# The edge matrix of a graph network, built in 56 groups of 14 packets of edges in place of 98 groups of 8

## What is computed

```python
edge_index = jnp.stack([src, dst])
h = relu(layernorm(x)); x = x + L0(h, edge_index, ...)      # two attention (GAT) layers, 4 heads
h = relu(layernorm(x)); x = x + L1(h, edge_weight, ...)     # 3 Lanczos steps: w = segment_sum(edge_weight * v[src], dst)
h = relu(layernorm(x)); x = x + L2(h, src, dst, ...)        # 3 SAGE layers: mean of h[src] over dst
h = relu(layernorm(x)); x = x + L3(h, edge_index, edge_type_16, ...)   # message passing with types
```

## Time and profile before

| | |
|---|---|
| median of 3 runs | 6159.81 us (6158.36 to 6174.29) |
| the profiled execution, its own time | 6145.26 us |
| its span, first to last instruction | 6143.5 us |
| mean granted TensorE clock | 0.691 |
| busy share of the span: PE, DVE, ACT, POOL | 50%, 51%, 29%, 62% |
| scatter of the matrix: first and last start | 234.3 and 1932.5 us |
| masks of the first attention layer | 1936 to about 2298 us |

### The profile page before, as it was taken

How to read it: one execution, slowest core, us unless ns; L and a number is a source line. 1 busy time by engine, 2 the same in 40 slices (tenths; PEclk the granted TensorE clock), 3 DMA queues, 4 the chain that set the end, 5 groups by cost and what they waited for, 6 DMA issues and landing times.

```text
span 6143.5 us, 54878 instructions
## 1 busy us (share of the span) xinstructions
PE 3078.6 (50%) x14893; PEld 1695.4 (28%) x14894; DVE 3122.8 (51%) x4163; ACT 1760.1 (29%) x2530; POOL 3806.0 (62%) x2603
## 2 busy tenths in 40 slices
PE   1311111111112556776434777699999934444444
PEld 0211111111111222221333222244445413333333
DVE  5455555444444998998798999611210051111111
ACT  0000000000001447998443999600111150000001
POOL 0377777777777888888787999810000007777774
PEclk6555555555555778999655999899999965555555
DMA  9422112222224974433897333487567642222222
GB/s 410 136 1 1 0 0 1 1 1 1 1 1 139 353 278 114 107 99 77 275 312 235 101 104 89 120 279 276 203 229 256 230 171 52 52 52 52 52 52 40
DMA packets 445350, 760.69 MB, mean 124 GB/s; under 512 B 273431, under 2 KB 351449, under 8 KB 405461
## 3 DMA queue, kind: packets, MB, share of 16 engines
q1 hardware_dynamic: 275280, 702.23, 33.7%
q0 software_dynamic: 163840, 54.71, 9.6%
q10 hardware_dynamic: 6146, 2.68, 0.2%
HBM read 552.67 MB, written 187.47 MB: 120 GB/s over the span
## 4 chain that ended last, share of the span: by engine, by line
issue 22%; PE 20%; POOL 18%; DVE 16%; DMA 15%; ACT 3%; POOLq 1%; SPq 1%; DVEq 0%; ACTq 0%
PE PS L636 17%; POOL edge_weight_and_count L579 12%; DVE tiles L1494 6%; POOL tiles L610 6%; DMA edge_weight_and_count<-weight_and_count,target 5%; DVE feature_major L1440 4%; DMA tiles<-edge_weight_and_count 4%; DVE tiles L1487 3%; DMA copies_then_records<-edge_count 3%; DMA tiles<-message_table,gather_index 2%; PE PS L756 1%; PE PS L945 1%; DMA message_table<-tiles 1%; ACT copies_then_records L1070 1%; DVE smax L1449 0%
## 5 line engine op out<-in xcount | busy, mean ns | idle before, releaser
L599 POOL DMA_INDIRECT sorted_edges<-record_slot,place_slot x784 | 1557.4, 1987 | 294.2 <-issue 212.1
L579 POOL DMA_INDIRECT edge_weight_and_count<-weight_and_count,target x784 | 1240.8, 1583 | 682.0 <-issue 251.0
L610 POOL DMA_INDIRECT tiles<-message_table,gather_index x808 | 774.9, 959 | 1274.4 <-DMA message_table<-tiles 1028.4
L636 PE MATMUL PS<-tiles,node_major 128*128 128x448 f32 (+1 forms) x2100 | 810.5, 546 | 10.7 <-ACT node_major L1001 10.7
L945 PE MATMUL PS<-tiles 128*128 128x128 f32 x1616 | 492.0, 460 | 614.1 <-DMA tiles<-message_table,gather_index 614.0
L636 PE MATMUL PS<-tiles 128*64 128x392 f32 (+1 forms) x3200 | 649.5, 528 | 292.9 <-DVE tiles L1494 290.8
L1494 DVE SCALAR_TENSOR_TENSOR tiles<-tiles,copies_then_records 128x1568 f32<-128x1568 f32 (+1 forms) x400 | 698.6, 1780 | 34.8 <-ACT tiles L1104 22.0
L1440 DVE SCALAR_TENSOR_TENSOR feature_major<-tiles,s,feature_major 128x1600 f32<-128x1600 f32 (+3 forms) x384 | 679.3, 1839 | 40.1 <-ACT tiles L1057 40.1
L945 PEld LDWEIGHTS PS<-tiles 128*128 128x128 f32 x1616 | 374.9, 322 | 731.7 <-issue 731.7
L1641 DVE TENSOR_TENSOR tiles<-lane_row,edges 128x1024 f32<-128x1024 f32 x101 | 123.5, 1225 | 881.4 <-PE PS L945 871.5
L636 PEld LDWEIGHTS PS<-tiles,node_major 128*128 128x128 f32 (+1 forms) x2100 | 400.5, 193 | 398.2 <-issue 383.2
(11 more groups left out here) (246 smaller groups left out, 3640.1 us busy)
## 6 DMA issues: line engine op xcount, KB each, us to landing
tiles<-edge_weight_turned SPq DMA_DIRECT2D x72, 1568.0 KB, 7.5
tiles<-edge_count SPq DMA_DIRECT2D x72, 1568.0 KB, 7.0
tiles<-edge_weight_and_count SPq DMA_DIRECT2D x48, 1600.0 KB
edge_weight_and_count<-tiles SPq DMA_DIRECT2D x48, 1568.0 KB, 39.3
copies_then_records<-edge_count SPq DMA_DIRECT2D x192, 392.0 KB
tiles<-edge_weight_and_count SPq DMA_DIRECT2D x48, 1536.0 KB, 8.7
edge_weight_turned<-copies_then_records SPq DMA_DIRECT2D x48, 768.0 KB, 4.8
edge_count<-copies_then_records SPq DMA_DIRECT2D x24, 800.0 KB, 4.1
```

Of the source, the lines that this page charges most:

```text
L579: nc.gpsimd.indirect_dma_start(out=edge_d, out_offset=bass.IndirectOffsetOnAxis(ap=idx[:, s, a:a + 1], axis=0), in_=pay[:, s, a, :], in_of ...
L599: nc.gpsimd.indirect_dma_start(out=rec_d, out_offset=bass.IndirectOffsetOnAxis(ap=place_slot[:, s, a:a + 1], axis=0), in_=rec_slot[:, s, a ...
L610: nc.gpsimd.indirect_dma_start(out=msg[:, s, a, :], out_offset=None, in_=table_d, in_offset=bass.IndirectOffsetOnAxis(ap=gs[:, s, a:a + 1] ...
L636: return nc.tensor.matmul(out_ap, lhsT, rhs, start=start, stop=stop)
```

## The change

The group size GB becomes 14 in all these places: 56 groups of 14 packets in place of 98 of 8. EC is still 784, so the 784 indirect DMAs of the matrix and the 784 of the sort stay. In a group the blocks are 14 * 15 / 2 = 105 in place of 36.

To fit two slots into the arrays, the blocks are stored as a folded triangle: row b (14 - b blocks) and row 13 - b (b + 1 blocks) share one strip of 15 blocks. The diagonal blocks then lie in two regular patterns, so the mask multiply becomes two instructions of 7 blocks each (`e.per = g + 2` signals a group in place of g + 1). One slot takes all of what was spare in `feature_major` from column 3 * 3136, the other starts at the front of `tiles`; so the zero tile, which SP reads while the first groups are made, moves to the array `Dinv`.

In PSUM a slot has four banks (1792 columns of keys, then `counted` and `summed` in the last 256 columns of its fourth bank). Packets 12 and 13 of a group's keys share that bank with the results of the group that used the slot before. So `key_rows` waits ahead of packet 12 for `edge_targets` of that group, and the tail waits for ScalarE's copy (`e.copied`) ahead of its first instruction in place of its third.

```diff
-GB, GM, GS = 8, 2, 8
+GB, GM, GS = 14, 2, 8
...
+        half, row, d = g // 2, (g + 1) * TP, g * TP
+        n = half * row
+        self.per = g + 2
+        self.words = (n + 2 * d) // 2
+        self.start = [b * row if b < half else (g - 1 - b) * row + (b + 1) * TP for b in range(g)]
+        self.diagonal_slot = [b if b < half else half + g - 1 - b for b in range(g)]
...
+        e0 = 8 * NP - 3 * ecp - 3 * ecp // 2
...
-        build_s = EdgeSteps(GB, [fm[0:TP, e1 + 3 * ecp // 2:8 * NP], tiles[0:TP, NP:3 * NP]], BF16, upto_b,
+        build_s = EdgeSteps(GB, [fm[0:TP, 3 * NP:e0], tiles[0:TP, :]], BF16, upto_b,
...
-        turned_keys = [bigT[0:TP, 8 * s:8 * s + 8, 0:TP] for s in range(2)]
-        counted = [BIG[0:TP, 6, 0:GB], SM[0:TP, 0:GB]]
+        turned_keys = [PS[0:TP, 4 * s:4 * s + 4, :].rearrange("p b (q n) -> p (b q) n", n=TP)[:, 0:GB, :] for s in range(2)]
+        counted = [PS[0:TP, 4 * s + 3, 256:256 + GB] for s in range(2)]
+        summed = [PS[0:TP, 4 * s + 3, 320:320 + 4 * GB] for s in range(2)]
...
-                    sp.dma_start(edge_m[t * TP:t * TP + n, k * NP:(k + 1) * NP], A[0][0:n, :]).then_inc(S("edges_cleared"), 16)
+                    sp.dma_start(edge_m[t * TP:t * TP + n, k * NP:(k + 1) * NP], Dinv[0:n, :]).then_inc(S("edges_cleared"), 16)
...
                 for a in range(e.g):
+                    if a == 12 and not (isinstance(i, int) and i < 2):
+                        pe.wait_ge(S(e.targets), i - 1 if isinstance(i, int) else before * 1)
                     last = nc.tensor.transpose(turned_keys[s][:, a, :],
...
-                    v.tensor_tensor(e.eqd[s], e.diagonal[s], e.upto[:, :].unsqueeze(1).to_broadcast([TP, e.g, TP]),
-                                    ALU.mult).then_inc(S(e.eq_done), 1)
+                    half = e.g // 2
+                    for k in range(2):
+                        v.tensor_tensor(e.eqd[s][:, k * half:(k + 1) * half, :], e.diagonal[s][k],
+                                        e.upto[:, :].unsqueeze(1).to_broadcast([TP, half, TP]), ALU.mult).then_inc(S(e.eq_done), 1)
...
+                    dve.wait_ge(S(e.copied), i + 1)
                     o(v.tensor_tensor(jk[:, s, 0:e.g], same[:, s, 0:e.g], counted[s][:, 0:e.g], ALU.subtract))
                     o(v.scalar_tensor_tensor(jk[:, s, 0:e.g], jk[:, s, 0:e.g], 1.0, junkD[:, at], ALU.min, ALU.mult))
-                    dve.wait_ge(S(e.copied), i + 1)
```

More of the change, by code:

```diff
@@ L158, in __init__, with columns @@
         self.targets, self.copied, self.added = targets, copied, added
[L159 to L162, removed]
+        half, row, d = g // 2, (g + 1) * TP, g * TP
[4 more added lines that the diff above has]
+        self.diagonal_slot = [b if b < half else half + g - 1 - b for b in range(g)]
+        self.flat, self.diagonal, self.eqd = [], [], []
         for a in areas:
-            a = a[:, 0:self.words] if dt == F32 else a[:, 0:self.words].bitcast(dt)
-            self.eq.append(a[:, 0:n].rearrange("p (b n) -> p b n", b=g))
-            self.diagonal.append(a[:, 0:n + d].rearrange("p (b n) -> p b n", b=g)[:, :, 0:TP])
+            a = a[:, 0:self.words].bitcast(dt)
+            self.flat.append(a[:, 0:n])
+            self.diagonal.append([a[:, 0:n].rearrange("p (i n) -> p i n", n=row)[:, :, 0:TP],
+                                  a[:, d:d + half * d].rearrange("p (i n) -> p i n", n=d)[:, :, 0:TP]])
             self.eqd.append(a[:, n + d:n + 2 * d].rearrange("p (b n) -> p b n", b=g))
+    def columns(self, s, b, first, last):
+        return self.flat[s][:, self.start[b] + (first - b) * TP:self.start[b] + (last - b) * TP]
 def graph_layers(nc, x, src, dst, etype, eweight, W1, as1, ad1, b1, W2, as2, ad2, b2, LW,
@@ L672, in to_feature_major, with key_rows @@
                 last.then_inc(S("fm_turned"), 1)
-            def key_rows(i, s, e):
+            def key_rows(i, s, e, before=None):
                 pe.wait_ge(S(e.loaded), i + 1)
                 for a in range(e.g):
+                    if a == 12 and not (isinstance(i, int) and i < 2):
+                        pe.wait_ge(S(e.targets), i - 1 if isinstance(i, int) else before * 1)
                     last = nc.tensor.transpose(turned_keys[s][:, a, :],
@@ L694, in sum_values @@
                     for b in range(a + 1):
-                        last = mm(BIG[0:TP, 4 + s, a * width:(a + 1) * width], e.eq[s][:, b, a * TP:(a + 1) * TP],
+                        last = mm(summed[s][:, a * width:(a + 1) * width], e.columns(s, b, a, a + 1),
                                   value(b), b == 0, b == a)
@@ L1304, in equal @@
                     for b in range(e.g):
[L1305 removed]
+                        v.tensor_scalar(e.columns(s, b, b, e.g).rearrange("p (a n) -> p a n", n=TP),
                                         turned_keys[s][:, b:e.g, :], ks[:, s, b:b + 1], None,
                                         ALU.is_equal, ALU.add, accum_out=same[:, s, b:b + 1]).then_inc(S(e.eq_done), 1)
[L1308 to L1310 removed]
+                    dve.wait_ge(S(e.eq_done), i * e.per + e.g)
+                    half = e.g // 2
+                    for k in range(2):
+                        v.tensor_tensor(e.eqd[s][:, k * half:(k + 1) * half, :], e.diagonal[s][k],
+                                        e.upto[:, :].unsqueeze(1).to_broadcast([TP, half, TP]), ALU.mult).then_inc(S(e.eq_done), 1)
                 def body(i, s, first):
```

21 lines of the change are left out of this document (11 added, 10 removed).

## The result

The changed kernel takes 6136.2 us (median of 20 runs, 6097 to 6171) where the kernel before takes 6190.0 (20 runs, 6150 to 6229, these beside it). The ratio is 0.9919, 95% interval 0.9900 to 0.9937: by the ratio 50 us, or 0.8%, faster, and 54 between the medians. Forecast was 42.

A forecast was written before the change was run, and what follows sets the result against it. GpSimd's scatter packets and the landing waits between groups were taken as the bound. Fewer group changes -86.5, later first group +22.5 and collisions +22 gave -42 us: 6118 us on the 6159.8 median, range 6086 to 6152.

The forecast's parts named there:

- What bounds the stage: Matrix scatter, 234 to 1933 us: GpSimd's packets and landing waits set the time; other engines cost nothing unless they delay GpSimd.
- the 40 us that the sum for the stage before left over: Scatter before: time beyond packets and group changes, put down to long gaps (21 us) and bucket work (15 us).
- Changes of group: GpSimd's scatter: 42 fewer group changes, each 2.06 us more than a packet inside a group, so -86.5 us.
- the long gaps: Scatter: about every 60 packets a gap inside a group is 1.96 us, not 0.30; 21 us in all, taken as staying.
- The first group: Ahead of the scatter's first packet: more key rows and two wider `equal` preparations delay it to about 257 us, +22.5.
- VectorE's idle for packets 12 and 13: Key rows in groups without bucket work: VectorE idles 0.9 us at the new wait for two transposes.
- Collisions: Scatter packets meeting mask multiplies in groups with bucket work: 21 packets held 1.05 us, +22; bounds 0 and 64.
- my law: Scatter packet needs something VectorE holds 0.13 us after its start, and waits until a running two-input multiply ends.
- collisions in both kinds of group: Rival: multiplies hold packets in groups with and without bucket work; -12 us, 6148 us, chance 0.15.
- The landing takes longer: Rival: the gap between groups is a backlog growing with packets; +55 us, 6215 us, chance 0.04.
- VectorE becomes the bound: Rival: wider comparisons make VectorE's group longer than GpSimd's 28.1 us; +31 us, 6191 us, chance 0.04.
- No collisions: Rival: mask multiplies hold no scatter packet; -64 us, 6096 us, chance 0.25.

The follow-up runs named there:

- hold_all: Changed kernel with the new wait moved from ahead of packet 12 to ahead of the first key-row transpose; one run, 6111.3 us, stage 1620.4 us.
- early_tail: Changed kernel with the tails of groups 0 and 1 ahead of the next group's preparation; ratio to the kernel before 0.9972, scatter ends at 1864.9 us.
- group4: Changed kernel with groups of 4 in place of 14, so 196 groups; ratio to the kernel before 1.0199, stage 1888.0 us.
- early_again: Repeat of early_tail on another chip, beside the changed kernel; ratio to the kernel before 0.9893, scatter ends at 1865.3 us.
- two_inputs: Changed kernel plus, in each group, one VectorE multiply of 3136 columns with two SBUF inputs; one run, 6235.9 us, stage 1701.6 us.
- psum_input: Changed kernel plus, in each group, two VectorE instructions of 1568 columns from PSUM to SBUF; one run, 6150.3 us, stage 1629.1 us.
- layout8: Changed kernel's new layout with groups of 8 in place of 14; ratio to the kernel before 0.9964, stage 1699.2 us.
- groups14_again: Changed kernel timed again unaltered, beside early_again; ratio to the kernel before 0.9907, scatter ends at 1876.2 us.

## Why the prediction was right, and where it was not

- **What bounds the stage**: shown. GpSimd's packets and landings set it; 270 us more VectorE work, 53 us more TensorE work, and 77 us more VectorE waiting (hold_all) change nothing. Of the 40 us that the sum for the stage before left over, the forecast named 21 and 15; the packets' own times over 1.56 each are 18 and not 15, and the rest, some 1 us, is in the rounding of the 0.30.
- **Changes of group, -86.5**: measured -80.9 in the gaps between packets (the stage is 79.6 us shorter, and the packets' own times are 1.3 us longer). The landing costs the same after 4, 8 and 14 packets. The term was too large by 5.6 us, since I took the long gaps as untouched by the grouping: five more of the same gaps now stand inside a group, where they add 1.6 us and not the 0.7 that they add on a change of group.
- **The first group, +22.5**: measured +23.3. The pitch of 0.14 us and 0.134 for 128 columns held for wider comparisons: 2.01 us from the one of 1792 columns to the next (timeline below). early_tail shows that the second `equal` stands in this path, for 13.4 us. The same kernel gave +22.0 in its second trace.
- **VectorE's idle for packets 12 and 13, 0.9**: measured 0.78.
- **Collisions, +22** (21 packets held for 1.05 us): the step that failed. The packets' own times grew by 1.3 us, and only one packet was clearly held by the multiplies, for 0.38 us (below). With bucket work the time of the multiplies was right to 0.1 us, and the law of who is held was not. Without bucket work the time was 0.19 us off where the margin was 0.05; by my law those packets would have been held too, which is the rival of collisions in both kinds of group, at -12. That it didn't happen is again the law.
- **The landing takes longer** and **VectorE becomes the bound**: fell, by group4 and hold_all.

The likeliest case was the wrong one of the list. *No collisions* was forecast at -64, by its terms, and the end of the scatter is at -56. As the collision term and the long gaps err in opposite ways, the forecast of -42 lies nearer to the measured -50 than its reasons earn. That is luck. The difference of 6 us between the scatter's 56 and the 50 of the ratio is inside the interval (39 to 62 us).

The changed kernel with bucket work, VectorE and GpSimd, beside the earlier trace rows:

```profile
1011.61 1.93 POOL L590 DMA_INDIRECT edge_weight_and_count<-weight_and_count,target  x1 [2.35 <-DMA edge_weight_and_count<-weight_and_count,target]
...
1013.84 1.60 POOL L590 DMA_INDIRECT edge_weight_and_count<-weight_and_count,target  x1 [0.30 <-issue]
...
1015.74 1.79 POOL L590 DMA_INDIRECT edge_weight_and_count<-weight_and_count,target  x1 [0.30 <-issue]
1016.74 2.08 DVE L1318 TENSOR_SCALAR_CACHE_REDUCE tiles<-PS,key_slot 128x1792 bf16<-128x1792 f32 x1 [0.65 <-DVE feature_major L1388]
...
1018.75 1.95 DVE L1318 TENSOR_SCALAR_CACHE_REDUCE tiles<-PS,key_slot 128x1664 bf16<-128x1664 f32 x1
...
1032.74 1.56 POOL L590 DMA_INDIRECT edge_weight_and_count<-weight_and_count,target  x1 [0.30 <-issue]
1032.80 1.16 DVE L1324 TENSOR_TENSOR tiles<-tiles,upto_b 128x896 bf16<-128x896 bf16 x2
```

The multiplies start 21.19 us behind the group's first packet (21.10 by the forecast) and a packet starts 0.06 us ahead of them. By my law it needs its index at 0.13 us, finds the multiply running, and takes 2.6 us. It takes 1.56. A group without bucket work, beside the earlier trace rows:

```profile
1040.23 0.69 PE L691 MATMUL PS<-consts,key_slot 128*128 128x128 f32 x2 [22.16 <-DVE target L1339]
1040.25 1.56 POOL L590 DMA_INDIRECT edge_weight_and_count<-weight_and_count,target  x1 [2.22 <-DMA edge_weight_and_count<-weight_and_count,target]
...
1040.96 2.08 DVE L1318 TENSOR_SCALAR_CACHE_REDUCE feature_major<-PS,key_slot 128x1792 bf16<-128x1792 f32 x1 [0.78 <-PE PS L691]
...
1042.96 1.95 DVE L1318 TENSOR_SCALAR_CACHE_REDUCE feature_major<-PS,key_slot 128x1664 bf16<-128x1664 f32 x1
...
1057.01 1.21 DVE L1324 TENSOR_TENSOR feature_major<-feature_major,upto_b 128x896 bf16<-128x896 bf16 x2
1057.02 1.56 POOL L590 DMA_INDIRECT edge_weight_and_count<-weight_and_count,target  x1 [0.30 <-issue]
...
1058.88 1.56 POOL L590 DMA_INDIRECT edge_weight_and_count<-weight_and_count,target  x1 [0.30 <-issue]
```

Here the multiplies start 16.76 us behind the first packet (16.95 by the forecast), 0.01 us ahead of a packet, and again it takes 1.56. In the cases from before VectorE's instruction had always begun ahead of the packet, by 0.16 us, 0.42 and 0.63. So they fit my law, and they fit another one as well: that the instruction which begins first holds the other. The two differ only for an instruction that begins about together with the packet, and the changed kernel has that in most of its groups. For 50 of its 57 pairs of multiplies a packet starts within 0.35 us of the first, with the multiply never more than 0.04 us ahead, and the packet takes 1.56 to 1.58. In 38 of the 50 it starts at most 0.08 us ahead of the multiply or 0.04 behind, where my law has it held. In one pair the multiply is clearly ahead of the packet:

```profile
1727.31 1.16 DVE L1324 TENSOR_TENSOR tiles<-tiles,upto_b 128x896 bf16<-128x896 bf16 x2
...
1727.43 1.94 POOL L590 DMA_INDIRECT edge_weight_and_count<-weight_and_count,target  x1 [0.30 <-issue]
```

The multiply (two in a row, 0.62 us each, 0.55 apart) begins 0.12 us ahead, the packet takes 0.38 us too long: it waits for the end of the first of the two, less 0.13, not of both. My forecast had them hold as one. In the traces a packet is held if the instruction with two SBUF inputs begins some 0.05 us or more ahead of it (0.047 us ahead held in early_again, 0.044 did not in two_inputs), for its remaining time less 0.13 us; two_inputs shows the size with one instruction of 3.4 us. A second input is not needed: the first packet of the earlier trace rows starts 0.16 us into a one-input fp32 instruction from SBUF to SBUF (L1370, 0.63 us) and takes 1.90, as the same sum gives. What GpSimd takes at its start was not tried apart from that.

The Trainium skill, "SBUF — State Buffer", section "Who interferes with whom", says that the order of issue, and not the kind of operation, decides who blocks. The traces agree as to the order: ahead by 0.09 us a multiply holds the packet (psum_input), and where the two start within 0.02 us of each other, the multiply ahead, the multiply is the one that is longer, by 0.05 us. Its remark that a tensor_tensor did not stall DMA descriptors does not hold for these indirect DMAs: 82 us in two_inputs, under a tensor_tensor.

## What to carry to other kernels

Where a stage is a chain of transfers that must land before the next batch, count batches: the time is packets times their price plus changes times the landing's latency, and work on other engines can grow by a third unseen as long as it is ready one batch ahead. Look at the start of the pipeline too: a larger batch is prepared as a whole before the first transfer, and early_tail gets half of that back by another order. Where the time of later stages spreads by more than the gain, compare spans without these stages, and say on which chip whole times don't follow the stage. Where a collision decides between instructions that start within 0.1 us of each other, a forecast needs cases of both orders, or it should give the two outcomes the same chance.

## What the runs showed of the hardware

- One VectorE instruction with two inputs in SBUF that runs when GpSimd begins an indirect DMA holds it until its end less 0.13 us, if it began some 0.05 us or more ahead: 3.02 to 4.73 us for a packet in place of 1.56 under an instruction of 3.4 us (two_inputs). A one-input fp32 instruction from SBUF to SBUF does it too (1.90 us). Instructions that read PSUM and write SBUF hold nothing (packets of 1.56 us beside 3.6 us of them a group, psum_input).
- At every 60th and every 113th packet GpSimd's gap inside a group is 1.9 us in place of 0.30. In before and in the changed kernel they stand at the same packets, 60, 113, 180, 226, 300, 339 and on, but for those that fall on a change of group. The cause is open.
- The kernel before took 6190 us on two sets of runs and 6355 on another chip, that of layout8, group4 and early_tail. There the part behind the second attention took 2362 to 2365 us in the three profiled executions, and 2225 to 2231 in the seven others; its gathers moved 45 to 47 GB/s there, 52 elsewhere. Ratios are within one chip.
- One attention took from 589 us (granted clock 0.945) to 646 (0.821) in nine profiled executions. Without the two attentions, three executions with groups of 14 (changed, groups14_again, hold_all) agree within 5 us, where their whole spans are 52 us apart.
